# Score matmuls of the last stage in eight 64x32 tiles instead of four 128x32 tiles

## The reference, cut to what matters

```python
def local_attention(q, k, v):            # 16 heads of 64, windows of w = 32 tokens
    bq, bk, bv = (t.reshape(b, h, n // w, w, d) for t in (q, k, v))
    bk2, bv2 = look(bk), look(bv)        # each window sees itself and the one before it
    mask = (it < jb) | (it > jb + w) | (jb == -1)
    sim = jnp.einsum('bhwie,bhwje->bhwij', bq, bk2) * QK_SCALE
    sim = jnp.where(mask, -jnp.finfo(sim.dtype).max, sim)
    attn = jax.nn.softmax(sim, -1)
    return jnp.einsum('bhwij,bhwje->bhwie', attn, bv2)

for i in range(6):
    x = attn_layer(shift_tokens(x), Wqkv[i], q_scale[i], k_scale[i], Wo[i]) + x
    x = ffn_layer(shift_tokens(x), ln_g[i], ln_b[i], W1[i], b1[i], W2[i], b2[i]) + x
```

## Time and profile before

| | us |
|---|---|
| median of three runs | 4433.01 |
| the profiled execution | 4435.17 |
| its span, first to last instruction | 4433.4 |
| PE busy | 4006.5 (90% of the span) |
| DVE busy | 3553.1 (80%) |
| ACT busy | 2545.2 (57%) |
| POOL busy | 2360.5 (53%) |

### The profile page before, as it was taken

The page is one execution under the profiler, slowest core; times in us unless marked ns, Lnnn a source line. Parts: engine busy times, 40 slices in busy tenths (PEclk is TensorE's granted clock), DMA queues, the critical chain, the costliest instruction groups (busy, mean ns, idle before and its releaser), DMA issues.

```text
span 4433.4 us, 119210 instructions
## 1 busy us (share of the span) xinstructions
PE 4006.5 (90%) x47524; PEld 2668.7 (60%) x47524; DVE 3553.1 (80%) x5486; ACT 2545.2 (57%) x5303; POOL 2360.5 (53%) x2019
## 2 busy tenths in 40 slices
PE   3335998999998699999999999999999999999997
PEld 1112444666666466666676766666666766666665
DVE  6775113666666799999999999989999899989996
ACT  2332333666665466666666666666666666666665
POOL 0001000000000587787788777877788777878874
PEclk7667999999999799999999999999999999999999
DMA  3000000000000233333333243234233243233333
GB/s 99 0 0 0 0 0 1 1 0 0 0 0 5 59 94 78 69 68 80 87 72 78 61 99 78 67 70 99 64 76 77 61 100 74 63 79 69 68 78 77
DMA packets 264304, 238.62 MB, mean 54 GB/s; under 512 B 31493, under 2 KB 259978, under 8 KB 263050
## 3 DMA queue, kind: packets, MB, share of 16 engines
q1 hardware_dynamic: 263818, 231.76, 22.4%
HBM read 26.13 MB, written 4.19 MB: 7 GB/s over the span
## 4 chain that ended last, share of the span: by engine, by line
PE 42%; DVE 23%; issue 10%; ACT 5%; SPq 1%; POOL 1%; DMA 1%; DVEq 0%; ACTq 0%; POOLq 0%
PE bank L1509 8%; PE bank L1576 6%; PE bank L1636 5%; PE bank L1594 5%; DVE arena L1105 4%; DVE arena L1068 4%; PE bank L1549 4%; DVE arena L1111 2%; PE bank L854 2%; PE bank L819 2%; PE bank L843 2%; DVE x_split L1050 2%; DVE arena L1124 2%; ACT arena L753 2%; PE bank L832 2%
## 5 line engine op out<-in xcount | busy, mean ns | idle before, releaser
L1068 DVE TENSOR_TENSOR arena<-bank,tab 128x1024 f32<-128x1024 f32 x768 | 935.4, 1218 | 152.9 <-ACT arena L1281 79.5
L1434 POOL TENSOR_TENSOR arena<-arena 128x512 f32<-128x512 f32 x768 | 1010.1, 1331 | 57.4 <-DMA arena<-arena 57.4
L1281 ACT ACTIVATE arena<-bank 128x512 f32<-128x512 f32 x768 | 458.5, 597 | 564.9 <-PE bank L1509 554.7
L1576 PE MATMUL bank<-m_vo,arena 128*32 128x512 f32 x6144 | 755.6, 598 | 13.8 <-DVE arena L1162 9.6
L1509 PE MATMUL bank<-x_split,wqk_split 128*128 128x256 f32 x4608 | 719.9, 299 | 53.1 <-DVE arena L1068 46.7
L1509 PEld LDWEIGHTS bank<-x_split,wqk_split 128*128 128x128 f32 x4608 | 604.7, 191 | 201.2 <-issue 109.6
L1442 POOL TENSOR_TENSOR arena<-arena 128x256 f32<-128x256 f32 x768 | 557.5, 737 | 144.1 <-ACT arena L1281 143.5
L1305 ACT ACTIVATE arena<-bank 128x512 f32<-128x512 f32 x768 | 458.8, 597 | 250.7 <-PE bank L1576 250.0
L1460 POOL MEMSET arena<- 128x4608 f32 x1 | 3.9, 3946 | 1039.4 <-DVEq L150 1039.4
L1451 POOL TENSOR_TENSOR arena<-arena 128x1024 f32<-128x1024 f32 x192 | 376.9, 1963 | 311.0 <-DVE arena L1117 311.0
L1457 POOL TENSOR_TENSOR arena<-arena 128x1024 f32<-128x1024 f32 x192 | 373.6, 1946 | 132.8 <-DVE arena L1130 132.8
(11 more groups left out here) (236 smaller groups left out, 7057.0 us busy)
## 6 DMA issues: line engine op xcount, KB each, us to landing
arena<-arena SPq DMA_DIRECT2D x1536, 128.0 KB, 2.5
wqk_stage<-in_wqk SPq DMA_DIRECT2D x6, 1024.0 KB, 7.9
out_x<-x_all SPq DMA_DIRECT2D x8, 512.0 KB, 4.9
wvt<-in_wvt SPq DMA_DIRECT2D x6, 512.0 KB, 4.2
wo<-in_wo SPq DMA_DIRECT2D x6, 512.0 KB, 5.4
arena<-in_wbh SPq DMA_DIRECT2D x1, 2048.0 KB, 9.4
arena<-out_x SPq DMA_DIRECT2D x4, 512.0 KB, 5.9
w<-in_w SPq DMA_DIRECT2D x6, 341.0 KB, 6.0
```

Source lines behind the costliest of these rows:

```text
L1068: nc.vector.tensor_tensor(d_t[c % KS].rearrange("p k h t -> p k (h t)"), bank[c % 2][:, :].unsqueeze(1).to_broadcast([P, 2, 2 * T]), tab[: ...
L1281: nc.scalar.activation(d_sq[i % 4].rearrange("p h t -> p (h t)"), bank[c % 2][:, :], ACT.Square).then_inc(s_sq, 1)
L1434: nc.gpsimd.tensor_tensor(d_rot[i // 4][:, i % 4, :, :], t[:, :, 0, :], t[:, :, 1, :], ALU.add).then_inc(s_ad, 1)
L1576: last = nc.tensor.matmul(bank[U_BANK[w]][g * WIN:(g + 1) * WIN, :], d_xt[n % 3][:, w * WIN:(w + 1) * WIN], m_vo[:, 4 * g:4 * g + 4, :].re ...
```

## The change

`scores` splits each product by head. The two heads of a pair go to two row tiles of the array, rows 0 to 63 and 64 to 127, and each writes a bank of its own (bank 2 and bank 3). With four tiles of 32 columns that is eight tiles. The mask goes the same way, eight matmuls over 64 rows each. A matmul has 64 columns now instead of 128, and there are 64 for a half instead of 32. `d_k` loses its zero halves. The banks now hold head by pair by window, and `scale_shifted`, `attention` and the layout of `mask_bf` follow. The DMAs that place queries and keys write other partitions in the same sizes.

```diff
-        d_k = ld(2, 4, 2, WIN + T)
+        d_k = ld(2, 4, WIN + T)
...
-                e = d_e[h].rearrange("p (w r) k -> p w r k", w=WPT)
-                factor = d_rq[:, WPT * h:WPT * h + WPT, :].rearrange("p w (r m) -> p w r m", m=8)[:, :, :, 4:5]
-                nc.gpsimd.tensor_tensor(e, e, factor.to_broadcast([P, WPT, QUADS, 2 * WIN]), ALU.mult).then_inc(s_rm, 1)
+                e = d_e[h].rearrange("p (r w) k -> p r w k", w=WPT)
+                factor = d_rq[:, WPT * h:WPT * h + WPT, :].rearrange("p w (r m) -> p r w m", m=8)[:, :, :, 4:5]
+                nc.gpsimd.tensor_tensor(e, e, factor.to_broadcast([P, QUADS, WPT, 2 * WIN]), ALU.mult).then_inc(s_rm, 1)
...
-                for b in range(2):
-                    for g in range(4):
-                        nc.tensor.matmul(bank[2 + b][g * WIN:(g + 1) * WIN, :], ident_bf[:, g * WIN:(g + 1) * WIN],
-                                         mask_bf[:, min(h + b, 1), :, :].rearrange("p a k -> p (a k)"),
-                                         start=True, stop=True, skip_group_check=True, tile_position=(0, g * WIN))
-                    for v in range(2):
-                        at = (4 * h + 2 * b + v) * WIN
-                        for a in range(2):
-                            for g in range(4):
-                                last = nc.tensor.matmul(bank[2 + b][g * WIN:(g + 1) * WIN, (2 * v + a) * P:(2 * v + a + 1) * P],
-                                                        d_q[:, a, g, at:at + WIN], d_k[:, a, g, :, at:at + 2 * WIN],
-                                                        start=False, stop=True, skip_group_check=True, tile_position=(0, g * WIN))
+                for g in range(4):
+                    for rr in range(2):
+                        pair = slice(rr * DH, rr * DH + DH)
+                        nc.tensor.matmul(bank[2 + rr][g * WIN:(g + 1) * WIN, :], ident_bf[pair, rr * DH:rr * DH + WIN],
+                                         mask_bf[pair, h, :, :].rearrange("p a k -> p (a k)"),
+                                         start=True, stop=True, skip_group_check=True, tile_position=(rr * DH, g * WIN))
+                for a in range(2):
+                    for w in range(WPT):
+                        at = (WPT * h + w) * WIN
+                        to = (a * WPT + w) * 2 * WIN
+                        for g in range(4):
+                            for rr in range(2):
+                                pair = slice(rr * DH, rr * DH + DH)
+                                last = nc.tensor.matmul(bank[2 + rr][g * WIN:(g + 1) * WIN, to:to + 2 * WIN],
+                                                        d_q[pair, a, g, at:at + WIN], d_k[pair, a, g, at:at + 2 * WIN],
+                                                        start=False, stop=True, skip_group_check=True, tile_position=(rr * DH, g * WIN))
                 last.then_inc(s_s, 1)
...
-                            at = (v * QUADS + r) * 2 + z
+                            at = (r * WPT + v) * 2 + z
...
-                    at = r % 2 * DH + h * WIN
-                    sp.dma_start(d_k[at:at + WIN, r // 2, :, r % 2, WIN:], d_rot[0][r * WIN:(r + 1) * WIN, :, h, :]).then_inc(s_dk, 16)
+                    at = r // 2 * DH + h * WIN
+                    sp.dma_start(d_k[at:at + WIN, r % 2, :, WIN:], d_rot[0][r * WIN:(r + 1) * WIN, :, h, :]).then_inc(s_dk, 16)
...
-                    at = r % 2 * DH + h * WIN
-                    sp.dma_start(d_q[at:at + WIN, r // 2, :, :], d_rot[1][r * WIN:(r + 1) * WIN, :, h, :]).then_inc(s_dq, 16)
+                    at = r // 2 * DH + h * WIN
+                    sp.dma_start(d_q[at:at + WIN, r % 2, :, :], d_rot[1][r * WIN:(r + 1) * WIN, :, h, :]).then_inc(s_dq, 16)
```

More of the change, by code:

```diff
@@ L1829, in _ @@
             nc.vector.tensor_copy(ident_bf[:, :], ident[:, :]).then_inc(const_ready, 1)
-            for t, at, many in ((1, 0, 8), (0, 4, 4)):
-                nc.vector.tensor_copy(mask_bf[:, t, at:at + many, :], mask_stage[:, 1, :].unsqueeze(1).to_broadcast([P, many, 2 * WIN]))\
-                    .then_inc(const_ready, 1)
-            nc.vector.tensor_copy(mask_bf[:, 0, 0:4, :], mask_stage[:, 0, :].unsqueeze(1).to_broadcast([P, 4, 2 * WIN]))\
-                .then_inc(const_ready, 1)
+            for t in range(TPS):
+                nc.vector.tensor_copy(mask_bf[:, t, :, :].rearrange("p (a w) k -> p a w k", w=WPT)[:, :, 1 - t:, :],
+                                      mask_stage[:, 1, :].unsqueeze(1).unsqueeze(1).to_broadcast([P, 2, WPT - 1 + t, 2 * WIN])).then_inc(const_ready, 1)
+            nc.vector.tensor_copy(mask_bf[:, 0, :, :].rearrange("p (a w) k -> p a w k", w=WPT)[:, :, 0, :],
+                                  mask_stage[:, 0, :].unsqueeze(1).to_broadcast([P, 2, 2 * WIN])).then_inc(const_ready, 1)
             nc.vector.memset(ones_row[:, :], 1.0).then_inc(const_ready, 1)
```

## The result

| | before | after |
|---|---|---|
| median, runs taken side by side | 4433.06 us (4432.02 to 4435.25) | 4500.22 us (4498.0 to 4501.7) |
| ratio | | 1.015, 95% interval [1.0133, 1.0168] |
| span of the profiled execution | 4433.4 us | 4497.7 us |
| from chunk 3's product in the first turn to that in the 96th | 2874.2 us | 2940.4 us |

The forecast was 4389 us with a range up to 4437: wrong, and wrong in the sign. The change costs 67 us. The last line is worked out from the starts of DVE's product of chunk 3 (L1068); 66 us of the 67 lie in it, so the last stage's turns alone hold the loss.

What follows compares the result with a forecast made beforehand. The prediction took DVE as the clock of the last stage's turns; 38 us from its waits for squares plus 5 us at layer starts made 43 us, giving 4392 us profiled and a 4389 us median, range 4360 to 4437.

Steps and rivals of the forecast that it cites:

- Path: Last stage's turns: shorter first-half scores remove DVE's waits for the squares of chunks 6 and 7; 43 us with layer starts.
- Length of a half: Scores of one half: 2.29 us before, taken as 1.25 us after, a gain of 1.04 us.
- the upper bound: Scores: PE starts instructions 5 ns apart, 0.08 us a group, so 1.61 us a half, a gain of 0.68 us.
- I cost it at nothing: Instruction fetch: 256 added PE instructions a turn mean one packet more, 4.5 instead of 3.5, taken as zero cost.
- first rival: The rival "PE cannot be fed", which noted that a packet of 256 takes 1.1 us, about as long as a half.
- PE cannot be fed: Scores: 27 ns a matmul is PE's own pace, so a half takes 3.7 us; 4568 us, chance 0.12.
- Keys: DVE's wait for POOL and the keys stays near 7.9 us in ten turns.
- Exactly one packet more leaves the phase as it was: Instruction queue: one added packet a turn keeps the alternation of turns with late matmuls and late keys; costed at nothing.

Runs made afterwards that it cites:

- half_products_8_tiles: The changed kernel with the products of the second pair of each chunk left out, 896 PE instructions a turn as before; 4396.7 us, 0.991 of the kernel before.
- in_phase_cheap_fill: Against the kernel before: first half in eight tiles, packet boundaries held in place by filling (bf16 ahead of the stage), weight loads spread; 4403.0 us, ratio 0.9933.
- the shifted kernels: Changed kernel with only the first half in eight tiles, plus 64, 128 or 192 PE instructions ahead of the last stage; 4454.2, 4446.6 and 4465.8 us.
- before_shift_64: The kernel before with 64 PE instructions of small f32 matmuls ahead of the last stage's turns; 4440.0 us, ratio 1.0018.

## Why the prediction was wrong

- **Path: right.** The forecast of 43 us for scores that take little time stands beside 36 to 41 us measured in `half_products_8_tiles`, DVE's wait for the squares fell there from 4.4 to 0.5 us in ten turns, and PE waited for DVE before its projections as it should.
- **Length of a half: the upper bound was right, not the value taken.** I took 1.25 us, by columns (0.055 us a group); measured are 1.46 us, that is 0.22 for the masks and 16 groups of 78 ns. This is the rate of starts, 16 x 5 ns, which I had as the other bound of the products and set aside because its twelve starts shared their window with a wait. The change of tile shape before the masks did not show in it. The gain of a half against before (2.09 us, measured in the same way) is 0.63 us, and not 1.04. In `in_phase_cheap_fill`, with one such half in a turn, 30 us were gained, of which about half stand in the wait for the squares.
- **"I cost it at nothing": the step that failed.** The prediction counted the packets rightly (45 in ten turns), and asked what they do to the keys. It did not ask whether they come in time for PE. The numbers were there: one packet for 249 instructions, about 1.1 us each, and 272 instructions in a half. It even wrote under its first rival that a packet takes about as long as a half would use its instructions. The missing piece was the time from PE's entering a block to the next one being there, 3.5 us in the median of the holes (1.0 to the packet's start, 2.5 from there), and that only one block is ahead. With it, a boundary costs about 3.5 us less the time in which PE uses up the block before it, and more where the packet is late. That is 141 us of idle time in place of the nothing in the forecast.
- **The rival "PE cannot be fed"** (0.12, 4568 us) named the right mechanism under another price. It put the loss into every matmul, with a half of over 2.3 us; in truth 130 of 192 halves are fast and 62 have a hole, and two fifths of the idle time are in `attention`, which has no more instructions than before. The pace of 25 ns a matmul that it took from the Trainium skill (TensorE: Matmul & The Clock Gate, section "Wait — 56ns, not 53.3ns?") is not what this trace shows for eight tiles together: 128 matmuls with their loads ran in 1.46 us, 11 ns each.
- **The sum.** The halves became 192 x 0.63 = 121 us shorter, and the holes are 141 us, 132 of them in the two lines. For PE that is nearly even. But only some 40 us of the first lay on the path, since the second half's scores are covered by DVE, while the holes fall in both halves and in `attention` as well. Over the 95 turns DVE waited 44 us more for the squares and 16 us more for the scores themselves (L1111), and 9 us less for the keys. How the 66 us divide between the two halves was not measured apart.
- **Keys.** "Exactly one packet more leaves the phase as it was" was true of the mean: the wait for the keys was 6.4 against 7.9 us in ten turns. That a packet among the keys' transfers costs about 1.1 us is supported by the shifted kernels, where one phase has that wait in every turn. `before_shift_64`, whose packets moved too, left it at 73 against 70 us over the 95 turns; its boundaries still change by half a block from turn to turn.

## What to carry to other kernels

Before cutting matmuls smaller, count the instructions, loads included, and compare the time of the densest 256 in a row with the time in which the next 256 come, here about 3.5 us from PE's entering a block and more behind other transfers. In this kernel smaller tiles gained only while that held. Where a short dense piece can't be avoided, its place against the boundaries can be worth as much as the edit itself (34 us between phases here) and can be set with a few cheap matmuls, and large loads should not be issued just before it.

## What the runs showed of the hardware

- PE's instructions come in packets of 16 KB for 256 of them. PE goes on 2.35 to 2.40 us after the start of a packet it waits for (four cases: 2577.10, 2612.33, 3001.00 and 3008.39 us), though these packets themselves take 0.9 to 1.0 us. Over 133 holes of the kernel after it is 2.2 to 2.9 us, and the packet starts 1.0 us (median) after PE enters the block before, in 39 cases over 2.5 us after.
- The packets share the DMA engines with data: behind the next layer's weights (1024, 512, 512 and 341 KB) one made a hole of 3.19 us, the longest holes were 3.7 us, and spreading these loads took 25 us off the changed kernel and nothing off the one before.
- Matmuls in eight tiles of 64x32 with 64 columns started at 5 ns for each load or matmul, 78 ns a group of eight, not at the 55 ns that the prediction worked out from columns.
- 86 bf16 matmuls of 32x32 ahead of the stage moved its start by 1.2 us, where 43 f32 matmuls over the whole array, with the same number of PE instructions, moved it by 16 to 18 us.
